# Row statistics of the second normalisation moved from the feed-forward stage into the attention stage, and two small steps of the feed-forward stage given to other engines

## The chip, the cores and the metric

The kernel runs on one core of a Trainium2 chip. The metric is the device time of one execution in microseconds, and lower is better. The kernel before takes 1919.89 us, the median of three runs (1918.67 to 1920.64).

## What is computed

64 images of 3x224x224 and 32 text tokens each are embedded, attended and passed through a feed-forward block:

```python
h = concat([patch_embed(x), text_embed(x_txt)])          # 64 x (196 + 32) x 192, float32
h = h + attention(layernorm(h))                          # 12 heads of 16, causal, q = k = v
h = h + bitlinear(gelu(bitlinear(layernorm(h), w1, g1)), w2, g2)    # 192 -> 768 -> 192

def bitlinear(x, w, g):
    xn = x * rsqrt(mean(x * x) + 1e-6) * g               # one root per row
    scale = 127 / clip(max(abs(xn)), 1e-5)               # one maximum per row
    xq = round(xn * scale) / scale                       # 8-bit values
    return xq @ ternary(w).T
```

The change concerns the last line of the model. Its first bitlinear needs, for every row of h, the mean and variance of the layernorm (the second one of the block), from which one root serves both the layernorm and the rmsnorm, and the largest absolute value of (h - mean) * g1. Its second bitlinear needs the sum of squares of the gelu's 768 outputs, a root of it, and their largest absolute value after g2.

## The kernel before

The rows h of all 64 images stay in SBUF (h_all). An image is 228 rows, held as two tiles of 112 and 116 partitions. The program has a setup, then an **attention stage** over the images, then a **feed-forward stage** over the images; the second starts when the last image's attention is added (semaphore s_h2). There is no scheduler: every engine runs its own list, written out by hand as a function step_images or ffn_step for one image, unrolled at both ends and put in a loop of two images in between. An engine takes its list strictly in order, so an instruction that waits holds up all behind it.

**Attention stage.** Step n of each engine works on four images at once: scores and values of image n, queries of n+1, patch statistics and first layernorm of n+2, patch matmuls of n+3, and the projection of n-1.
- PE (step_images from L1240 on): scores 0, square_turn (L1135, releases DVE's front), queries, scores 1, project(n-1), scores 2, values 0 and values 1 (L1228), a piece of the patches (L1072), score rounds, and so on. values g waits until POOL has cleared the later keys of group g.
- DVE: front(n+2) (L682 to L716) with, inside it, normalise(n-1) (L748), the split of the queries (L725, L727) and add_attention(n-1) (L754); then three maxima (L738) and the reciprocal of the denominators (L743).
- POOL: patch_roots (L454), clear_later of group 0 (L469, two instructions), sides (L435, L438), clear_later of group 1, norm_roots (L459), clear_later of group 2, add_squares (L449, four instructions).

**Feed-forward stage.** Step i of each engine:
- DVE ffn_step (L807 to L874), for image m = i+1: bn_stats and bn_aggr (L820, L824), the variance (L828), the centred and weighted rows v1 (L838), their maxima (L843); for image i-1 the mean of gelu squares (L832), the maxima of v2 (L857); for image i-3 the output rows (L850); then one chain of five small instructions for both quantisers (L863 to L867), each waiting for the one ahead, and last the rounding of v1 to q1 (L874).
- ACT: copy of the turned q1 (L1015), both tiles of q2 (L1003), gelu (L1024), copy of the turned q2 (L1032), squares of the gelu (L1038).
- POOL: one root of four numbers per row, for both normalisations (L512), then g2 times gelu in eight instructions (L524).
- PE: turn_first (L1303), ffn_second (L1333) of image i-2, ffn_first (L1314) of i+1, turn_second (L1325) of i-1.

Of the kernel before, what the change touches and what calls it, by code (L numbers as in the profile page):

```python
# [9 lines left out]
ALU = mybir.AluOpType  # L10
# [29 lines left out]
READY1, READY2 = 36, 52  # L40
# [12 lines left out]
def build(nc, x, x_txt, gamma, beta, tok_w, tok_b, table, pos, carry, qkv_w, qkv_b,  # L53
          proj_w, proj_b, w1, g1, w2, g2, cf, cb, out):
    ctx = ExitStack()
    with ctx:
# [28 lines left out]
        ln_st = sb("ln_st", [128, 32])  # L85
# [69 lines left out]
        v1 = part(xpix[0][:, :], 384, 2 * DIM).rearrange("p (t d) -> p t d", t=2)  # L155
# [73 lines left out]
        f_var = sem("mean_squares_ready")  # L229
        f_r1 = sem("inverse_roots_ready")  # L230
        f_q1 = sem("first_quantised")
# [7 lines left out]
        f_q2 = sem("second_quantised")  # L239
# [15 lines left out]
        V_SETUP, T_SETUP = 69, 9  # L255
# [162 lines left out]
        def _(pool):  # L418
# [42 lines left out]

            zero = pool.to_reg(0.0)
# [32 lines left out]

            step_images(-2, 1, 1, old=False)
            step_images(-1, 0, 2, old=False)
            step_images(0, 1, 2)
            step_images(1, 0, 3)
# [6 lines left out]
            step_images(IMAGES - 1, 0, None, newer=False, newest=False)  # L506

            def ffn_step(i, b, new=True, mid=True):

                if new or mid:  # L510
                    pool.wait_ge(f_var, i + 2)
                    nc.gpsimd.tensor_tensor(ff_st[:, b, 20:24], ff_st[:, b, 16:20], expo[:, 0:4],  # L512
                                            ALU.pow).then_inc(f_r1, 1)
                if not (isinstance(i, int) and (i < 0 or i >= IMAGES)):
                    after(pool, f_q2, i - 1)
                    for tile, P in enumerate((TA, TB)):
                        pool.wait_ge(f_g, 2 * i + tile + 1)
                        if tile == 0:
                            pool.wait_ge(f_r1, i + 2)
                        else:  # L520
                            pool.wait_ge(f_v2, 2 * i + 1)
                        for lo in range(0, HIDDEN, HIDDEN // 4):
                            cols = slice(lo, lo + HIDDEN // 4)
# [10 lines left out]
            with pool.Fori(2, PAIRS - 1) as t:  # L534
                for b in range(2):
                    ffn_step(2 * t + b, b)
# [882 lines left out]
```

## Time and profile before

| | |
|---|---|
| median of three runs | 1919.89 us |
| the profiled execution | 1918.11 us, of which the span of its instructions is 1916.4 us |
| busy share of the span | PE 84%, DVE 72%, ACT 61%, POOL 57% |
| PE in 40 slices (tenths) | 0539999999999999999999999999556666666666 |
| DVE in 40 slices | 3635666666666666666666666666289999999996 |
| POOL in 40 slices | 5035555555555555555555555554177777777775 |
| granted TensorE clock | 1.0 of full speed in the attention stage, a mean of 0.65 in the feed-forward stage |

How to read it: each digit of the slices is the busy share of 1/40 of the span, in tenths (9 is 90% or more). Setup ends near 100 us, the attention stage near 1389 us, and the rest is the feed-forward stage. DVE is the VectorE, ACT the ScalarE, POOL the GpSimd engine, PE the TensorE; PEld is PE's loading of weights, which overlaps the matmuls. An engine's busy share says how much work it has, not whether it sets the pace: for that one looks at who waits for whom.

### The profile page before, as it was taken

Reading aid. Unit: us, or ns where it says so; the run is one execution under the profiler, and the core shown is the slowest. Engines: PE = TensorE matmul, PEld = TensorE weight load, DVE = VectorE, ACT = ScalarE, POOL = GpSimd, SP = SyncE. Lnnn points to the kernel's source line nnn. Section 1 sums busy time; section 2 is a strip of 40 time slices with the busy share of each in tenths; the row PEclk is TensorE's granted clock in tenths of the full one; section 3 lists DMA queues with packets and bytes.
Section 4 is the critical chain, followed back from the end, with each engine's and each line's share of the span. In section 5 each row is a group of like instructions: output and inputs, shape, how many; then the busy total and the mean of one; then the engine's idle time right before and its main releaser. Section 6 shows DMA issues by size and latency. Waiting matters only on the chain.

```text
span 1916.4 us, 50514 instructions
## 1 busy us (share of the span) xinstructions
PE 1614.7 (84%) x16574; PEld 1363.0 (71%) x16574; DVE 1371.2 (72%) x3151; ACT 1171.3 (61%) x1830; POOL 1089.9 (57%) x1503
## 2 busy tenths in 40 slices
PE   0539999999999999999999999999556666666666
PEld 0438888888888888888888888887445555555555
DVE  3635666666666666666666666666289999999996
ACT  1124555555555555555555555555278888888887
POOL 5035555555555555555555555554177777777775
PEclk9969999999999999999999999999666666666665
DMA  8564656565656565656565656561000000000000
GB/s 103 137 116 69 100 78 99 79 100 78 100 79 100 78 99 80 100 79 99 80 100 78 99 80 100 79 99 26 24 12 22 22 22 22 22 22 22 22 22 26
DMA packets 159967, 132.96 MB, mean 69 GB/s; under 512 B 32558, under 2 KB 151040, under 8 KB 159808
## 3 DMA queue, kind: packets, MB, share of 16 engines
q1 hardware_dynamic: 159168, 131.00, 44.0%
q0 software_dynamic: 768, 1.57, 0.5%
q8 instruction: 17, 0.28, 0.1%
q14 instruction: 14, 0.11, 0.0%
HBM read 118.32 MB, written 11.91 MB: 68 GB/s over the span
## 4 chain that ended last, share of the span: by engine, by line
PE 70%; DVE 14%; issue 5%; SPq 4%; ACT 3%; DMA 2%; POOL 1%; DVEq 1%; ACTq 0%; POOLq 0%
PE ps L1072 24%; PE ps L1154 8%; PE ps L1237 7%; PE ps L1228 7%; DVE ff_st L857 4%; PE ps L1184 4%; PE ps L1216 3%; PE ps L1189 3%; PE ps L1210 3%; PE ps L1314 3%; PE ps L1333 2%; DVE xpix L838 2%; PE ps L1145 2%; PE ps L1135 1%; PE ps L1168 1%
## 5 line engine op out<-in xcount | busy, mean ns | idle before, releaser
L1072 PE MATMUL ps<-w_eff,xpix 118*112 118x193 f32 (+1 forms) x2048 | 457.2, 362 | 21.0 <-POOL side L438 20.4
L1072 PEld LDWEIGHTS ps<-w_eff,xpix 118*112 118x112 f32 (+1 forms) x2048 | 387.8, 253 | 39.8 <-issue 32.8
L915 ACT ACTIVATE probs<-ps,isw 116x688 f32<-116x688 f32 x384 | 298.7, 830 | 175.6 <-PE ps L1216 175.6
L449 POOL TENSOR_TENSOR xsq<-xsq 118x784 f32<-118x784 f32 (+2 forms) x192 | 221.8, 1155 | 293.6 <-ACT xsq L909 283.5
L738 DVE TENSOR_REDUCE nmax<-ps 116x12 bf16<-116x1344 f32 (+2 forms) x192 | 302.2, 1574 | 108.7 <-PE ps L1189 103.8
L524 POOL TENSOR_TENSOR xpix<-probs,g_b 112x192 f32<-112x192 f32 (+1 forms) x512 | 296.5, 609 | 109.0 <-ACT probs L1024 99.7
L469 POOL TENSOR_SCALAR_AFFINE_SELECT probs<-probs 116x464 f32<-116x464 f32 x384 | 268.4, 717 | 46.5 <-ACT probs L915 31.0
L682 DVE TENSOR_SCALAR front_st<-ps 112x1 f32<-112x1 f32 (+1 forms) x128 | 18.3, 152 | 229.2 <-PE ps L1135 218.1
L1314 PE MATMUL ps<-w1t,xpix 96*112 96x384 f16 (+1 forms) x512 | 160.7, 488 | 14.5 <-ACT xpix L1015 13.3
L1154 PE MATMUL ps<-xnT,wq_pad 97*128 97x228 f32 (+1 forms) x768 | 166.0, 365 | 0.0
L1303 PE MATMUL ps<-ident_h,xpix 112*96 112x112 f16 (+1 forms) x256 | 34.9, 281 | 152.9 <-DVE xpix L874 152.9
L943 ACT ACTIVATE aux<-ps 128x344 bf16<-128x344 bf16 x64 | 29.3, 457 | 214.4 <-PE ps L1198 214.4
L1237 PE MATMUL ps<-wp_pad,aT 128*112 128x192 f32 (+1 forms) x768 | 144.5, 339 | 11.7 <-DVE aT L748 11.7
L454 POOL TENSOR_TENSOR front_st<-front_st,expo 128x2 f32<-128x2 f32 x64 | 45.0, 703 | 190.9 <-DVE front_st L690 179.1
L909 ACT ACTIVATE xsq<-xpix,consts 118x1176 f32<-118x1176 f32 x64 | 145.6, 2275 | 0.0
L1154 PEld LDWEIGHTS ps<-xnT,wq_pad 97*128 97x128 f32 (+1 forms) x768 | 142.2, 192 | 2.9
L1024 ACT ACTIVATE probs<-ps,ff_st 112x768 f32<-112x768 f32 (+1 forms) x128 | 112.9, 899 | 47.6 <-PE ps L1314 46.2
L1228 PE MATMUL ps<-probs,vaug 112*32 112x228 f32 (+1 forms) x3072 | 140.0, 314 | 2.1 <-POOL probs L469 1.3
L1303 PEld LDWEIGHTS ps<-ident_h,xpix 112*96 112x96 f16 (+1 forms) x256 | 23.8, 168 | 165.7 <-issue 95.8
L1314 PEld LDWEIGHTS ps<-w1t,xpix 96*112 96x112 f16 (+1 forms) x512 | 100.2, 206 | 54.4 <-issue 15.3
L1237 PEld LDWEIGHTS ps<-wp_pad,aT 128*112 128x112 f32 (+1 forms) x768 | 124.6, 182 | 16.0 <-DVE aT L748 12.0
L1333 PE MATMUL ps<-w2t,xpix 128*112 128x192 f16 (+1 forms) x768 | 121.4, 338 | 4.7 <-ACT xpix L1032 4.7
(160 smaller groups left out, 3393.3 us busy)
## 6 DMA issues: line engine op xcount, KB each, us to landing
xpix<-in_x SPq DMA_DIRECT2D x192, 196.0 KB
xpix<-in_x SPq DMA_DIRECT2D x192, 195.1 KB
rden<-den_rows SPq DMA_DIRECT2D x256, 85.5 KB, 2.2
out<-xpix SPq DMA_DIRECT2D x64, 87.0 KB
out<-xpix SPq DMA_DIRECT2D x64, 84.0 KB
xpix<-in_x SPq DMA_DIRECT2D x128, 34.1 KB
xpix<-in_x SPq DMA_DIRECT2D x128, 34.0 KB
den<-o_sb SPq DMA_DIRECT2D x256, 2.7 KB
```

The costliest lines, as they stand in the source:

```text
L449: nc.gpsimd.tensor_tensor(out_, a, b, ALU.add).then_inc(s_ssq, 1)
L469: nc.gpsimd.affine_select(both, both, [[0, 2], [0, 2], [1, TB]], ALU.is_ge, zero, base=0, channel_multiplier=-1).then_inc(s_causal, 1)
L524: last = nc.gpsimd.tensor_tensor(v2[0:P, b, tile, cols], gel[0:P, b, tile, cols], g2_b[0:P, cols], ALU.mult)
L738: V.tensor_reduce(dst, src, AX_X, ALU.max, negate=True).then_inc(s_mx, 1)
L909: A(xsq[0:HI, 1:7, :], pixels[:, 1:7, :], ACT.Square, scale=mult_root[0:HI, 1:2]).then_inc(s_sq, 1)
L915: A(probs[0:TB, g, 2 * e:2 * e + 2, :], ps[0:TB, 4 + 2 * e:6 + 2 * e, 0:SK], ACT.Exp, scale=isw[0:TB, 7:8]).then_inc(s_p, 1)
L1072: last = MM(ps_tok[tile][0:P, :], src, w_eff[0:HI, o, :], start=(o == 0), stop=(o == OFFS - 1))
L1154: last = MM(ps_q[:, g, :], wq_pad[0:K, c, g, :], xnT[0:K, c, :], start=(c == 0), stop=(c == 1))
L1228: last = MM(ps_o[32 * j:32 * j + 32, g, lo:TOK], vaug[0:K, tile, PER * g + j, :], probs[0:K, g, j, at:end], start=(tile == 0), stop=(tile ...
L1237: last = MM(ps[0:P, 1, tile * 256:tile * 256 + DIM], aT[:, g, lo:lo + P], wp_pad[:, g, :], start=(g == 0), stop=(g == GROUPS - 1))
L1314: last = MM(ps[0:P, 2 + 2 * tile + half, 0:HIDDEN // 2], q1T[0:HALF, tile, c, 0:P], w1t[0:HALF, c, half * (HIDDEN // 2):(half + 1) * (HIDD ...
L1333: last = MM(ps[0:P, 1, tile * 256:tile * 256 + DIM], q2T[:, tile, c, 0:P], w2t[:, c, :], start=(c == 0), stop=(c == NCH - 1))
```

## The change

1. **In the attention stage** DVE ends each step with a new function measure(n-1): bn_stats, bn_aggr, the variance, a copy of the mean, the centred rows v1 and their maxima for the image whose attention has just been added. POOL gets row_roots(n-2), a root of two numbers, between patch_roots and the first clear_later.
2. **Between the stages** five small instructions on DVE work out the first quantiser's scales of all images at once.
3. **In the feed-forward stage** DVE no longer has L820, L824, L828, L832 and L843; v1 is computed again (centre), q1 is rounded before the second chain instead of behind it, and the chain is of two numbers per row instead of four. The second tile of q2 is rounded on DVE (quantise_second) instead of ACT. POOL adds the epsilon and takes the gelu's root itself, behind its eight products (gelu_roots); the division by 768 moves into ACT's squares as a scale. v1 gets a buffer of its own.

PE's list stays as it is, save that turn_second waits for the two tiles of q2 apart.

```diff
-            def step_images(n, par, count, old=True, newer=True, newest=True):
+            def step_images(n, par, count, prev=True, old=True, newer=True, newest=True):
                 if newer:
                     patch_roots(n + 2)
+                if prev:
+                    row_roots(n - 2)
                 if old:
                     clear_later(n, 0)
...
+            row_roots(IMAGES - 2)
+            row_roots(IMAGES - 1)
+
+            def weight(n, b):
+                after(pool, f_q2[0], n - 1)
+                after(pool, f_q2[1], n - 1)
+                for tile, P in enumerate((TA, TB)):
+                    pool.wait_ge(f_g, 2 * n + tile + 1)
+                    for lo in range(0, HIDDEN, HIDDEN // 4):
+                        cols = slice(lo, lo + HIDDEN // 4)
+                        last = nc.gpsimd.tensor_tensor(v2[0:P, b, tile, cols], gel[0:P, b, tile, cols],
+                                                       g2_b[0:P, cols], ALU.mult)
+                    last.then_inc(f_v2, 1)
+
+            def gelu_roots(n, b):
+                pool.wait_ge(f_ssq, 2 * n + 2)
+                apart(pool)
+                nc.gpsimd.tensor_scalar(ff_st[:, b, 18:20], gel_sum[:, b, :], EPS_RMS, None,
+                                        ALU.add).then_inc(f_var, 1)
+                pool.wait_ge(f_var, n + 1)
+                nc.gpsimd.tensor_tensor(ff_st[:, b, 20:22], ff_st[:, b, 18:20], expo[:, 0:2],
+                                        ALU.pow).then_inc(f_r1, 1)
+
...
+            for filled in (mean2, rms, peak):
+                step(V.memset(filled[:, :], 1.0))
...
+            def measure(n):
+
+                def chain(ins, k):
+                    ins.then_inc(s_mean2, 1)
+                    dve.wait_ge(s_mean2, n * 3 + k)
+
+                dve.wait_ge(s_h2, n + 1)
+                apart(dve)
+                for tile, P in enumerate((TA, TB)):
+                    last = V.bn_stats(ln_st[0:P, 20 + 6 * tile:26 + 6 * tile], h_all[0:P, hcols(n, tile)])
+                chain(last, 1)
+                apart(dve)
+                for tile, P in enumerate((TA, TB)):
+                    last = V.bn_aggr(ln_st[0:P, 34 + 2 * tile:36 + 2 * tile], ln_st[0:P, 20 + 6 * tile:26 + 6 * tile])
+                chain(last, 2)
+                after(dve, s_rms, n)
+                V.tensor_scalar(ln_st[:, 32:34], ln_st[:, 35:38:2], 1.0 + EPS_RMS,
+                                EPS_LN * EPS_RMS, ALU.mult, ALU.add).then_inc(s_var2, 1)
+                V.tensor_copy(mean2[:, bass.ds(n * 2, 2)], ln_st[:, 34:38:2])
+                for tile, P in enumerate((TA, TB)):
+                    last = V.scalar_tensor_tensor(v1[0:P, tile, :], h_all[0:P, hcols(n, tile)],
+                                                  ln_st[0:P, 34 + 2 * tile:35 + 2 * tile], g1_b[0:P, :],
+                                                  ALU.subtract, ALU.mult)
+                chain(last, 3)
+                for tile, P in enumerate((TA, TB)):
+                    last = V.tensor_reduce(peak[0:P, bass.ds(n * 2 + tile, 1)], v1[0:P, tile, :], AX_X, ALU.max,
+                                           apply_absolute_value=True)
+                last.then_inc(s_peak, 1)
...
+                if prev:
+                    measure(n - 1)
...
+            links[:] = [0, IMAGES * V_FRONT]
+            dve.wait_ge(s_peak, IMAGES)
+            dve.wait_ge(s_rms, IMAGES)
+            link(V.tensor_tensor(peak[:, :], rms[:, :], peak[:, :], ALU.mult))
+            link(V.tensor_scalar(peak[:, :], peak[:, :], 1e-5, None, ALU.max))
+            link(V.reciprocal(inv_peak[:, :], peak[:, :]))
+            V.tensor_scalar(step1[:, :], peak[:, :], isw[:, 4:5], None, ALU.mult)
+            link(V.scalar_tensor_tensor(scale1[:, :], inv_peak[:, :], 127.0, rms[:, :], ALU.mult, ALU.mult))
+            dve.sem_inc(f_sc1, 1)
+
+            F_LINKS = 4
...
+            def centre(n):
+
+                after(dve, f_q1, n)
+                for tile, P in enumerate((TA, TB)):
+                    ins = V.scalar_tensor_tensor(v1[0:P, tile, :], h_all[0:P, hcols(n, tile)],
+                                                 mean2[0:P, bass.ds(n * 2 + tile, 1)], g1_b[0:P, :],
+                                                 ALU.subtract, ALU.mult)
+                ins.then_inc(f_v1, 1)
...
+            def quantise_second(n, b):
+                dve.wait_ge(f_sc, n + 1)
+                after(dve, f_t2, n)
+                V.tensor_scalar(q2[0:TB, 1, :], v2[0:TB, b, 1, :], ff_st[0:TB, b, 39:40], MAGIC16, ALU.mult,
+                                ALU.add).then_inc(f_q2[1], 1)
...
+            def ffn_step(i, b, new=True, mid=True, last_=True):
+
+                if new:
+                    centre(i + 1)
+                if last_:
+                    final(i - 3, 1 - b)
+                if mid:
+                    peaks(i - 1, 1 - b)
+                if new:
+                    quantise_first(i + 1)
+                if mid:
+                    second_scales(i - 1, 1 - b)
+                    quantise_second(i - 1, 1 - b)
```

How the lists move at three places (rows of the programs' own order; a line number of the changed kernel lies some lines below that of the kernel before):

POOL, one attention step, before (front_st, ln_st and rms hold statistics, expo the exponent, probs the probabilities, side and xpix pixels):

```order
L454 TENSOR_TENSOR front_st<-front_st,expo 128x2
L469 AFFINE_SELECT probs<-probs 116x2x232 x2
L435 COPY side<-xpix 54x14x13
L438 COPY side<-xpix 54x14x13
L469 AFFINE_SELECT probs<-probs 116x2x232 x2
L459 TENSOR_TENSOR ln_st<-ln_st,expo 128x2
L469 AFFINE_SELECT probs<-probs 116x2x232 x2
```

and with the change:

```order
L466 TENSOR_TENSOR front_st<-front_st,expo 128x2
L476 TENSOR_TENSOR rms<-ln_st,expo 128x2
L486 AFFINE_SELECT probs<-probs 116x2x232 x2
L447 COPY side<-xpix 54x14x13
L450 COPY side<-xpix 54x14x13
L486 AFFINE_SELECT probs<-probs 116x2x232 x2
L471 TENSOR_TENSOR ln_st<-ln_st,expo 128x2
L486 AFFINE_SELECT probs<-probs 116x2x232 x2
```

The new root stands between the patch root and the first clearing.

DVE, the end of one attention step and the start of the next, with the change (before, L757 is followed at once by L701; nmax are the score maxima, v is v1, mean is mean2):

```order
L757 TENSOR_REDUCE nmax<-ps 116x4
L785 BN_STATS ln_st<-h_all 112x6
L785 BN_STATS ln_st<-h_all 116x6
L789 BN_AGGR ln_st<-ln_st 112x2
L789 BN_AGGR ln_st<-ln_st 116x2
L792 TENSOR_SCALAR ln_st<-ln_st 128x2
L794 COPY mean<-ln_st 128x2
L796 SCALAR_TENSOR_TENSOR v<-h_all,ln_st,g_b 112x192
L796 SCALAR_TENSOR_TENSOR v<-h_all,ln_st,g_b 116x192
L801 TENSOR_REDUCE peak<-v 112x1
L801 TENSOR_REDUCE peak<-v 116x1
L701 TENSOR_SCALAR front_st<-ps 112x1
```

The ten instructions from L785 to L801 were not there.

DVE, the end of one feed-forward step and the head of the next, before (xpix is v1 or q1, ff_st statistics):

```order
L874 TENSOR_SCALAR xpix<-xpix,ff_st 112x192
L874 TENSOR_SCALAR xpix<-xpix,ff_st 116x192
L820 BN_STATS ff_st<-h_all 112x6
L820 BN_STATS ff_st<-h_all 116x6
L824 BN_AGGR ff_st<-ff_st 112x2
L824 BN_AGGR ff_st<-ff_st 116x2
L828 TENSOR_SCALAR ff_st<-ff_st 128x2
L832 TENSOR_SCALAR ff_st<-gel_sum 128x2
L838 SCALAR_TENSOR_TENSOR xpix<-h_all,ff_st,g_b 112x192
L838 SCALAR_TENSOR_TENSOR xpix<-h_all,ff_st,g_b 116x192
L843 TENSOR_REDUCE ff_st<-xpix 112x1
L843 TENSOR_REDUCE ff_st<-xpix 116x1
```

and with the change (xpix<-v is q1, probs<-xpix is q2, xpix<-ps the output rows):

```order
L882 TENSOR_SCALAR xpix<-v,scale 112x192
L882 TENSOR_SCALAR xpix<-v,scale 116x192
L907 TENSOR_TENSOR ff_st<-ff_st 128x2
L908 TENSOR_SCALAR ff_st<-ff_st 128x2
L909 RECIPROCAL ff_st<-ff_st 128x2
L911 TENSOR_SCALAR ff_st<-ff_st,isw 128x2
L912 SCALAR_TENSOR_TENSOR ff_st<-ff_st 128x2
L918 TENSOR_SCALAR probs<-xpix,ff_st 116x768
L873 SCALAR_TENSOR_TENSOR v<-h_all,mean,g_b 112x192
L873 SCALAR_TENSOR_TENSOR v<-h_all,mean,g_b 116x192
L890 SCALAR_TENSOR_TENSOR xpix<-ps,ff_st,h_all 112x192
L890 SCALAR_TENSOR_TENSOR xpix<-ps,ff_st,h_all 116x192
```

Eight instructions (L820 to L832 and L843) are gone from the head of the step, the rounding of q1 (L882) has moved ahead of the chain, and the rounding of q2 (L918) stands at the end.

## Rows read from the trace of the kernel before

Times are microseconds from the start of the span unless marked ns. A timeline row gives start, length, engine, line, operation, output<-inputs, shapes, how many instructions were merged (xN), and in brackets how long the engine had been idle and what ended that.

**Rows 1.** Busy time, granted clock and DMA, two stretches (columns: PE, PEld, DVE, ACT, POOL, PEclk).
```profile
400.00:1300.00 900.00, 899.55 (x10378) 772.32 (x10375) 622.42 (x1269) 522.92 (x752) 499.78 (x658) 1.00 0.62 90
1450.00:1890.00 440.00, 300.95 (x1997) 245.14 (x1996) 404.40 (x1159) 380.61 (x662) 322.96 (x497) 0.65 0.07 22
```

**Rows 2.** The page, part 5: the values matmuls and who held them up.
```profile
L1228 PE MATMUL ps<-probs,vaug 112*32 112x228 f32 (+1 forms) x3072 | 140.0, 314 | 2.1 <-POOL probs L469 1.3
```

**Rows 3.** Timeline of POOL, one attention step (start, length in us).
```profile
1038.72 0.70 POOL L454 TENSOR_TENSOR front_st<-front_st,expo 128x2 f32<-128x2 f32 x1 [2.91 <-DVE front_st L690]
1039.39 1.81 POOL L469 TENSOR_SCALAR_AFFINE_SELECT probs<-probs 116x464 f32<-116x464 f32 x2
...
1041.93 0.49 POOL L438 COPY side<-xpix 54x182 f32<-54x182 f32 x1 [0.16 <-POOL side L435]
1042.66 1.15 POOL L469 TENSOR_SCALAR_AFFINE_SELECT probs<-probs 116x464 f32<-116x464 f32 x2 [0.24 <-POOL side L438]
```

**Rows 4.** Timeline of PE's weight loads, same step.
```profile
1043.27 0.57 PEld L1228 LDWEIGHTS ps<-probs,vaug 112*32 112x32 f32 x16
```

**Rows 5.** Timeline of DVE, end of one attention step and start of the next.
```profile
1033.30 1.05 DVE L738 TENSOR_REDUCE nmax<-ps 116x4 bf16<-116x912 f32 x1
1037.70 0.16 DVE L682 TENSOR_SCALAR front_st<-ps 112x1 f32<-112x1 f32 x1 [3.35 <-PE ps L1135]
...
1039.20 0.86 DVE L748 TENSOR_TENSOR aT<-o_sb,rden 128x684 f32<-128x684 f32 x1
1039.98 1.44 DVE L699 SCALAR_TENSOR_TENSOR h_all<-tok_t,front_st,bw 112x192 f32 x2
```

**Rows 6.** Timeline of POOL during DVE's gap.
```profile
1031.52 3.62 POOL L449 TENSOR_TENSOR xsq<-xsq 118x784 f32<-118x784 f32 x3 [4.38 <-ACT xsq L909]
1035.21 0.60 POOL L449 TENSOR_TENSOR ssq_sb<-xsq 118x196 f32<-118x196 f32 x1
```

**Rows 7.** Timeline of PE, feed-forward stage.
```profile
1599.66 2.80 PE L1314 MATMUL ps<-w1t,xpix 96*112 96x384 f16 x8 [0.92 <-ACT xpix L1015]
1602.26 1.35 PE L1325 MATMUL ps<-ident_h,probs 112*128 112x112 f16 x12
...
1613.10 0.61 PE L1303 MATMUL ps<-ident_h,xpix 112*96 112x112 f16 x4 [2.37 <-DVE xpix L874]
...
1615.43 1.85 PE L1314 MATMUL ps<-w1t,xpix 96*112 96x384 f16 x8
1617.12 0.77 PE L1325 MATMUL ps<-ident_h,probs 112*128 112x112 f16 x12
```

**Rows 8.** Timeline of ACT, feed-forward stage.
```profile
1611.07 1.37 ACT L1032 ACTIVATE xpix<-ps 128x672 f16<-128x672 f16 x2
...
1613.96 0.60 ACT L1015 ACTIVATE xpix<-ps 96x224 f16<-96x224 f16 x2
```

**Rows 9.** Timeline of DVE, one feed-forward step.
```profile
1605.42 0.60 DVE L820 BATCH_NORM_STATS2 ff_st<-h_all 112x6 f32 x2
...
1606.99 0.15 DVE L832 TENSOR_SCALAR ff_st<-gel_sum 128x2 f32<-128x2 f32 x1
...
1607.82 0.61 DVE L843 TENSOR_REDUCE ff_st<-xpix 112x1 f32<-112x192 f32 x2
```

**Rows 10.** Line L843: all its instructions, first and last start.
```profile
L843 DVE TENSOR_REDUCE ff_st<-xpix x128: 340/348/354, 1390.9 to 1887.1; 112x1 f32<-112x192 f32 x64, 116x1 f32<-116x192 f32 x64
```

**Rows 11.** Groups by line and shape, DVE, 1450 to 1890 us.
```profile
L874 DVE TENSOR_SCALAR xpix<-xpix,ff_st 112x192 f16<-112x192 f32 x55 | 31.3, 570 | 1.9
...
L874 DVE TENSOR_SCALAR xpix<-xpix,ff_st 116x192 f16<-116x192 f32 x55 | 16.9, 307 | 0.0
```

**Rows 12.** Timeline of DVE in the setup: the widest rounding to half precision.
```profile
75.64 0.76 DVE L631 TENSOR_SCALAR xpix<-xpix 128x1152 f16<-128x1152 f32 x1
```

**Rows 13.** Groups by line, POOL, 1450 to 1890 us.
```profile
L524 POOL TENSOR_TENSOR xpix<-probs,g_b 112x192 f32<-112x192 f32 (+1 forms) x442 | 255.6, 608 | 96.9 <-ACT probs L1024 89.0
L512 POOL TENSOR_TENSOR ff_st<-ff_st,expo 128x4 f32<-128x4 f32 x55 | 67.5, 1226 | 21.0 <-DVE ff_st L832 11.9 <-POOL xpix L524 9.1
```

More of the change, by code:

```diff
@@ L238, in build @@
         f_v2 = sem("gelu_weighted")
-        f_q2 = sem("second_quantised")
+        f_q2 = [sem(f"second_quantised{i}") for i in range(2)]
         f_t2 = sem("second_transposed")
@@ L506, in _ @@
             step_images(IMAGES - 1, 0, None, newer=False, newest=False)
[L508 to L523, printed above, removed]
-                            last = nc.gpsimd.tensor_tensor(v2[0:P, b, tile, cols], gel[0:P, b, tile, cols],
-                                                           g2_b[0:P, cols], ALU.mult)
-                        last.then_inc(f_v2, 1)
-                    pool.wait_ge(f_v2, 2 * i + 2)
@@ new lines, in gelu_roots @@
+            def gelu_roots(n, b):
[6 more added lines that the diff above has]
+                                        ALU.pow).then_inc(f_r1, 1)
+            weight(0, 0)
@@ L535, in _ @@
+            gelu_roots(0, 0)
+            weight(1, 1)
+            gelu_roots(1, 1)
+            with pool.Fori(1, PAIRS) as t:
                 for b in range(2):
-                    ffn_step(2 * t + b, b)
-            ffn_step(IMAGES - 2, 0)
-            ffn_step(IMAGES - 1, 1, new=False)
-            ffn_step(IMAGES, 0, new=False)
+                    weight(2 * t + b, b)
+                    gelu_roots(2 * t + b, b)
         @block.vector
@@ new lines, in centre, with quantise_first @@
+            def centre(n):
[5 more added lines that the diff above has]
+                ins.then_inc(f_v1, 1)
+            def quantise_first(n):
+                dve.wait_ge(f_v1, n + 1)
+                after(dve, f_t1, n)
+                for tile, P in enumerate((TA, TB)):
+                    ins = V.tensor_scalar(q1[0:P, tile, :], v1[0:P, tile, :], scale1[0:P, bass.ds(n * 2 + tile, 1)],
+                                          MAGIC16, ALU.mult, ALU.add)
+                ins.then_inc(f_q1, 1)
@@ new lines, in final, with peaks @@
+            def final(n, b):
+                dve.wait_ge(f_m2, n + 1)
+                after(dve, f_out, 32 * n)
+                for tile, P in enumerate((TA, TB)):
+                    end = V.scalar_tensor_tensor(y[0:P, tile, :], ps[0:P, 1, tile * 256:tile * 256 + DIM],
+                                                 ff_st[0:P, b, 42 + tile:43 + tile], h_all[0:P, hcols(n, tile)],
+                                                 ALU.mult, ALU.add)
+                end.then_inc(f_y, 1)
+            def peaks(n, b):
+                dve.wait_ge(f_v2, 2 * n + 2)
+                for tile, P in enumerate((TA, TB)):
+                    ins = V.tensor_reduce(ff_st[0:P, b, 26 + tile:27 + tile], v2[0:P, b, tile, :], AX_X, ALU.max,
+                                          apply_absolute_value=True)
+                flinks[:] = [0, n * F_LINKS]
+                flink(ins)
@@ L888, in _ @@
             ffn_step(IMAGES - 1, 1, new=False)
[L889 removed]
+            ffn_step(IMAGES, 0, new=False)
             ffn_step(IMAGES + 1, 1, new=False, mid=False)
```

136 lines of the change are left out of this document (46 added, 90 removed).

## The prediction

> **What bounds the kernel now.** I read the busy time by stage first, then who waits for whom, then one step of each stage in order of time. In the attention stage PE is busy 899.55 of 900 us at the full clock; DVE has 622 us of work there and POOL 500 [rows 1]. So PE sets the pace, work added to DVE or POOL is free as long as PE waits for none of it, and each us that PE waits per image costs about 60 us. In the feed-forward stage no engine is full: per 440 us DVE has 404, ACT 381, POOL 323, PE 301 at a mean clock of 0.65 [rows 1]. There DVE's step is what PE waits for: before turn_first it stands idle 2.37 us until L874 has written q1 [rows 7]. The step takes (1887.1-1390.9)/63 = 7.87 us, since L843 runs twice per image [rows 10].
>
> **The attention stage, POOL.** Today PE waits for POOL's clearings a total of 1.3 us in the run [rows 2], which looks like room and isn't. In the step shown, POOL starts the patch root at 1038.72 and ends the second clearing of group 1 at 1042.66+1.15 = 1043.81, with almost no idle time between [rows 3]. PE's 16 weight loads of values 0 end at 1043.27+0.57 = 1043.84, and those of values 1 need that clearing [rows 4]. The slack is 0.03 us. The new root goes between the patch root and the first clearing. It is the same instruction as the patch root, 0.70 us [rows 3]. Part of it is covered. The first pair of clearings takes 1.81 us where the second takes 1.15 [rows 3]: it overlaps DVE's L748 (1039.20 to 1040.06) and L699 (1039.98 to 1041.42, 1.44 us for two) [rows 5]. I read this as DVE and POOL taking turns at SBUF. The root too will wait for L748's end, so POOL is ready for the first clearing at about 1040.06+0.60 = 1040.65 instead of being let through at about 1040.0. By the same turns the pair ends some 0.7 later; a tenth I take off, since the sides behind it then meet none of L699. That makes 0.6 us of wait for PE per image. Ends: 0.45, if the pair, met by less of DVE's work, shrinks by another 0.15 towards 1.15; and 1.05, if POOL's root and DVE shut each other out wholly: L699's two instructions then start half a root, 0.35, later than with a clearing in their way, the clearings behind them too, and nothing is regained (0.70+0.35). I take the low part of that span because of the next row.
>
> L748 starts at 1039.20, inside the patch root (1038.72 to 1039.42), and takes 0.86 us for 684 elements a row, in line with L738's 1.05 for 912 (which reads no SBUF), so the root doesn't keep it out in its last 0.2 us [rows 3, 5]. The Trainium skill (SBUF — State Buffer, Who interferes with whom) says that DVE and GpSimd hold their shared port pair for a whole instruction, the other fully blocked. By that rule L699's first instruction waits for the whole new root, the clearing waits for L699, and the stage would lose the upper end. The trace does not agree for this root, as far as L748's 0.86 us show.
>
> The root meets patch_roots and the clearings in steps 2 to 61: 60 x 0.6 = +36 us (27 to 63).
>
> **The attention stage, DVE.** measure stands where DVE waits for PE: L738 ends at 1034.35, L682 starts at 1037.70, a gap of 3.35 us [rows 5]. Its instructions are those of the feed-forward head. There the head runs from L820's start at 1605.42 to L843's end at 1607.82+0.61 = 1608.43, 3.0 us with its waits for POOL [rows 9]; L832 goes out of it and the copy of the mean comes in, 0.1 each. So 3.0 us fit with 0.3 to spare. In the gap POOL runs its square sums until 1035.81 [rows 6]; DVE's variance may wait for the last of them. I count 0 for DVE. If measure took 3.9, the excess of 0.5 would go through the front, POOL's chain and the clearings to PE. POOL's square sums end 1.9 us before L682, which needs them through PE, so some tenths of delay there cost nothing.
>
> **The feed-forward stage, DVE.** Removed: the head up to L832's start, 1606.99-1605.42 = 1.57 us, L832's 0.15 and L843's 0.61, less 0.1 of overlap: 2.2 us [rows 9]. Added: q2's tile of 116x768. L874 on 192 elements takes 0.307 without a wait [rows 11], the setup's rounding of 1152 elements 0.76 [rows 12]; between them 768 gives 0.58. L874's first tile takes 0.570, 0.26 more than the second, which is the wait for POOL [rows 11]; so 0.85. DVE's own step becomes 7.87-2.2+0.85 = 6.5 us.
>
> **POOL.** Eight products of 0.608 are 4.9 us [rows 13]. The root of two numbers is 0.70 [rows 3] instead of 1.23 [rows 13]. The addition of an epsilon has no row on POOL. Below, zero; above, 0.60, the addition of 196 columns [rows 6]; three such additions of 784, 392 and 196 columns take 3.62 [rows 6], some 2 ns a column, so two columns cost about 0.2. With 0.3 for hand-overs POOL needs 6.1 us: no bound, even with 0.6 it is 6.5. What it does is add about 1 us to the way from the squares to q2's scales, which have a whole step of slack.
>
> **ACT and PE, late next.** The change leaves a loop untouched: q1's copy on ACT, ffn_first and turn_second on PE, q2's copy and the squares on ACT, next q1's copy. From the start of L1032 to the start of L1015 ACT needs 1613.96-1611.07 = 2.89 us, L1015 itself 0.60 [rows 8], the hand-over to PE 0.1. PE from L1314's start to L1325's end takes 1599.66 to 1603.61 = 3.95 us at half clock, and 1615.43 to 1617.89 = 2.46 where the clock rose to full in between [rows 7]. A mean of 0.65 is 30% of the time at full clock, giving 3.95x0.7+2.46x0.3 = 3.5. The loop is 2.89+0.60+0.1+3.5 = 7.1 us. That is the new step: the loop is longer than DVE's 6.5 and POOL's 6.1, and ACT, busy 381x7.87/440 = 6.8 us a step [rows 1], loses one of its eight long instructions. Ends: 7.54 with the half clock throughout, and 6.5, DVE's own. Gain: 64 x (7.87-7.1) = -49 us (-21 to -88).
>
> **Edges.** Three fills in the setup, 0.4 us. Between the stages the last measure (3.0) and five chained small instructions (0.16 each as L682 [rows 5], 0.9 with hand-overs) come before the first q1, where the head of image 0 was; the second q1 then follows faster. The last image waits 1 us longer for POOL and saves half of ACT's rounding. Together +0.5.
>
> **Sum.** 36-49+0.5 = -12.5 on the profiled execution's 1918.1: 1905.6. The median of the runs is 1.8 above it, so 1907. A measurement of this kernel can tell about 0.2% (4 us) from no change.
>
> **Rivals.**
> - *PE waits longer in attention* (slower). POOL's root and L699 exclude each other, or measure outgrows its gap of 3.35 us. From a wait of 0.81 us on, the stage's loss exceeds the other's gain. With 1.05: 63-49+0.5 = +14, or 1934. For: slack of 0.03 us and DVE within 0.3 of its gap. Against: L748 wasn't held up by the patch root. Chance 0.22.
> - *The loop at half clock* (slower). The stage's step is 7.54, the gain 21: +36-21 = +15, or 1935. For: PE would be busier at half clock, with no guarantee of more. Against: today's mean is 0.65. Chance 0.10.
> - *The stage runs at DVE's own 6.5.* The clock rises as PE's idle 2.37 us per step shrinks, and the loop gives way: 36-88 = -52, or 1868. For: the full clock where PE is never idle [rows 1]. Chance 0.13.
> - *The new root is hidden.* The clearings speed up enough that PE doesn't wait: -49, or 1871. Against it the slack of 0.03. Chance 0.08.
>
> **How the numbers follow.** The forecast has 0.47. The forecast's own range is 1892 to 1925 (a wait of 0.45 to 0.8 us, a step of 7.0 to 7.2). The range reaches to the slow cases with 3 us beyond, and to half of the fast ones: 1870 to 1938. Faster: 0.39 of the forecast, and both fast cases, 0.60. Within 0.2%: 0.08 of the forecast and 0.04 of the first rival, 0.12. Slower: the rest, 0.28.
>
> **What would show it.** In attention: PE idle before values 1 by 0.6 us, put down to POOL's clearing; DVE's wait before the front near 0.3 us instead of 3.35; POOL's new root at 0.7 us plus a wait. In the feed-forward stage: a step of 7.1, DVE with idle time of its own, and a granted clock of 0.65 or more. The prediction is wrong if PE doesn't wait in attention, or if the step's limit is POOL.

## The result and the profile after

The changed kernel takes 1938.6 us, the median of 4 runs (1937.7 to 1940.1), against 1919.5 for the kernel before on the same chip: a ratio of 1.010 (95% interval 1.008 to 1.012). It is slower by 19 us where 1907 had been forecast. The profiled execution's span grew from 1916.4 to 1936.2 us, 19.8 us. In the tables below "before" is measured anew on each chip, at 1918 to 1920 us.

Busy time and granted clock of the changed kernel, in the two stretches of [rows 1] (columns as there):

```profile
400.00:1300.00 900.00, 888.76 (x10167) 750.22 (x10167) 701.86 (x1703) 517.19 (x737) 508.07 (x690) 1.00 0.61 88
1450.00:1890.00 440.00, 262.72 (x1981) 217.75 (x1981) 415.13 (x773) 336.85 (x609) 329.30 (x555) 0.78 0.07 22
```

PE has lost 11 of its 900 busy us in the attention stage. In the feed-forward stage DVE is busier than before and PE less, at a granted clock of 0.78 where it had 0.65. Where the 19.8 us lie can be read from first and last starts. The rows are of single lines (busy ns least/median/most, then first and last start): the attention's normalising multiply in the kernel before and after (once per image), and the maxima of the feed-forward stage before and after (twice per image):

```profile
L748 DVE TENSOR_TENSOR aT<-o_sb,rden x64: 857/860/1131, 174.7 to 1383.7; 128x684 f32<-128x684 f32 x64
L857 DVE TENSOR_REDUCE ff_st<-xpix x128: 939/941/952, 1402.5 to 1902.8; 112x1 f32<-112x768 f32 x64, 116x1 f32<-116x768 f32 x64
```

```profile
L767 DVE TENSOR_TENSOR aT<-o_sb,rden x64: 857/861/1016, 175.4 to 1404.8; 128x684 f32<-128x684 f32 x64
L898 DVE TENSOR_REDUCE ff_st<-xpix x128: 932/941/954, 1425.3 to 1923.4; 112x1 f32<-112x768 f32 x64, 116x1 f32<-116x768 f32 x64
```

The attention stage grew from 1209.0 to 1229.4, +20.4 us. The feed-forward stage shrank from 500.3 to 498.1, only -2.2 us (the maxima follow each other at (498.1-0.9)/63 = 7.89 us, before 7.93; the prediction's 7.87 is the same step by another line). What lies ahead, between and behind adds 0.7+1.7-0.8 = +1.6.

**The attention stage.** POOL and DVE around the new root, the clearing that values 1 need, and PE's weight loads there (timeline of the changed kernel: start, length, what the engine was idle for):

```profile
1035.94 0.70 POOL L466 TENSOR_TENSOR front_st<-front_st,expo 128x2 f32<-128x2 f32 x1 [2.96 <-DVE front_st L709]
1036.61 1.21 POOL L476 TENSOR_TENSOR rms<-ln_st,expo 128x2 f32 x1
1037.78 1.15 POOL L486 TENSOR_SCALAR_AFFINE_SELECT probs<-probs 116x464 f32<-116x464 f32 x2
1038.89 0.48 POOL L447 COPY side<-xpix 54x182 f32<-54x182 f32 x1
...
1040.26 1.15 POOL L486 TENSOR_SCALAR_AFFINE_SELECT probs<-probs 116x464 f32<-116x464 f32 x2 [0.24 <-POOL side L450]
```

```profile
1036.35 0.86 DVE L767 TENSOR_TENSOR aT<-o_sb,rden 128x684 f32<-128x684 f32 x1
1037.13 0.74 DVE L718 SCALAR_TENSOR_TENSOR h_all<-tok_t,front_st,bw 112x192 f32 x2
```

```profile
1041.46 0.55 PEld L1280 LDWEIGHTS ps<-probs,vaug 112*32 112x32 f32 x16 [0.50 <-POOL probs L486]
```

The new root waits for L767 and takes 1.21 us. From the patch root to the first clearing there are now 1037.78-1035.94 = 1.84 us, where there were 0.67 [rows 3]: 1.17 more. The pair of clearings takes 1.15 instead of 1.81, since L718 now runs during the root and not during them. From the first pair's start to the second's there are 1040.26-1037.78 = 2.48 us, where there were 1042.66-1039.39 = 3.27 [rows 3]. So of the 1.17 us 0.79 come back, and the pair that values 1 need starts 0.38 us later behind the patch root than before. PE waits for it. In the middle of the stage (from the fifth start of the normalising multiply to the 61st, over 56) the step grew from 19.18 to 19.57 us, by just that 0.38; the steps at the ends lose less, and 20.4 us over 60 steps are 0.34 each.

DVE's added work did fit in its gap, as the step's end shows (0.39 us are left of the 3.35 of [rows 5]):

```profile
1031.36 0.61 DVE L785 BATCH_NORM_STATS2 ln_st<-h_all 112x6 f32 x2
...
1033.85 0.61 DVE L801 TENSOR_REDUCE peak<-v 112x192 f32 x2
1034.85 0.16 DVE L701 TENSOR_SCALAR front_st<-ps 112x1 f32<-112x1 f32 x1 [0.39 <-PE ps L1187]
```

**The feed-forward stage.** Here stands what the prediction did not have. L882 writes q1, and its first tile is one instruction on 192 columns. The group by shape, DVE, 1450 to 1850 us (busy, mean ns of one, idle before), and one stretch of all engines:

```profile
L882 DVE TENSOR_SCALAR xpix<-v,scale 112x192 f16<-112x192 f32 x51 | 96.9, 1901 | 14.9 <-DVE ff_st L898 14.9
L882 DVE TENSOR_SCALAR xpix<-v,scale 116x192 f16<-116x192 f32 x51 | 15.6, 306 | 0.0
```

```profile
1710.45 4.66 POOL L536 TENSOR_TENSOR xpix<-probs,g_b 112x192 f32<-112x192 f32 x8 [0.15 <-ACT probs L1075]
1711.42 2.70 DVE L882 TENSOR_SCALAR xpix<-v,scale 112x192 f16<-112x192 f32 x2 [0.29 <-DVE ff_st L898]
...
1714.17 0.61 PE L1355 MATMUL ps<-ident_h,xpix 112*96 112x112 f16 x4 [3.58 <-DVE xpix L882]
```

The first tile takes 1901 ns in the mean, the second 306; before they took 570 and 307 [rows 11]. Here the pair starts at 1711.42, while POOL's second product of eight runs, and ends at 1714.12, when POOL is in its seventh; PE idles 3.58 us for it, where it idled 2.37 before [rows 7]. One image in three escapes (0.63 us for the tile), and there the step is 7.0 us; in the others, with 2.5 to 2.7 us for the tile, it is 8.3 to 8.6. Called "hold-out" below: an instruction of DVE that is kept waiting while several of POOL's pass.

### The profile page after: what moved, and what is told of

It reads as the page before. It is cut to its first block, busy times and chain, and to the rows that moved or that the text cites. A ratio compares the mean times of both kernels' runs of the same rounds, so it can differ in the third digit from the quotient of the medians.

```text
span 1936.2 us, 51421 instructions
## 1 busy us (share of the span) xinstructions
PE 1582.7 (82%) x16574; PEld 1325.7 (68%) x16574; DVE 1508.7 (78%) x3341; ACT 1126.5 (58%) x1766; POOL 1121.9 (58%) x1629
## 4 chain that ended last, share of the span: by engine, by line
issue 30%; PE 29%; POOL 17%; DVE 14%; SPq 4%; DMA 2%; POOLq 2%; ACT 2%; DVEq 1%; ACTq 0%
PE ps L1124 13%; POOL probs L486 6%; POOL xsq L461 5%; DVE ff_st L898 4%; PE ps L1280 3%; PE ps L1236 2%; PE ps L1385 2%; PE ps L1366 2%; PE ps L1241 2%; POOL side L450 2%; POOL side L447 1%; DVE v L873 1%; DVE xpix L890 1%; DVE ff_st L908 1%; DVE xpix L882 1%
## 5 line engine op out<-in xcount | busy, mean ns | idle before, releaser
L757 DVE TENSOR_REDUCE nmax<-ps 116x12 bf16<-116x1344 f32 (+2 forms) x192 | 302.7, 1577 | 140.9 <-PE ps L1241 134.1
L536 POOL TENSOR_TENSOR xpix<-probs,g_b 112x192 f32<-112x192 f32 (+1 forms) x512 | 314.8, 650 | 118.4 <-ACT probs L1075 117.2
L486 POOL TENSOR_SCALAR_AFFINE_SELECT probs<-probs 116x464 f32<-116x464 f32 x384 | 230.0, 616 | 25.9 <-POOL side L450 14.6
L1280 PE MATMUL ps<-probs,vaug 112*32 112x228 f32 (+1 forms) x3072 | 151.1, 315 | 15.8 <-POOL probs L486 15.8
L1366 PE MATMUL ps<-w1t,xpix 96*112 96x384 f16 (+1 forms) x512 | 134.7, 424 | 24.7 <-ACT xpix L1067 24.7
L1075 ACT ACTIVATE probs<-ps,step 112x768 f32<-112x768 f32 (+1 forms) x128 | 110.6, 898 | 73.3 <-PE ps L1366 73.3
L882 DVE TENSOR_SCALAR xpix<-v,scale 112x192 f16<-112x192 f32 (+1 forms) x128 | 129.9, 1054 | 17.2 <-DVE ff_st L898 17.0
L1366 PEld LDWEIGHTS ps<-w1t,xpix 96*112 96x112 f16 (+1 forms) x512 | 86.4, 177 | 55.4 <-issue 22.1
```

Source lines behind the costliest of these rows:

```text
L486: nc.gpsimd.affine_select(both, both, [[0, 2], [0, 2], [1, TB]], ALU.is_ge, zero, base=0, channel_multiplier=-1).then_inc(s_causal, 1)
L536: last = nc.gpsimd.tensor_tensor(v2[0:P, b, tile, cols], gel[0:P, b, tile, cols], g2_b[0:P, cols], ALU.mult)
L757: V.tensor_reduce(dst, src, AX_X, ALU.max, negate=True).then_inc(s_mx, 1)
L882: ins = V.tensor_scalar(q1[0:P, tile, :], v1[0:P, tile, :], scale1[0:P, bass.ds(n * 2 + tile, 1)], MAGIC16, ALU.mult, ALU.add)
L1280: last = MM(ps_o[32 * j:32 * j + 32, g, lo:TOK], vaug[0:K, tile, PER * g + j, :], probs[0:K, g, j, at:end], start=(tile == 0), stop=(tile ...
L1366: last = MM(ps[0:P, 2 + 2 * tile + half, 0:HIDDEN // 2], q1T[0:HALF, tile, c, 0:P], w1t[0:HALF, c, half * (HIDDEN // 2):(half + 1) * (HIDD ...
```

## The experiments

Three theories were open. T1: POOL's new root costs the attention stage its 20 us. T2: the hold-out of q1's first tile eats the gain of the feed-forward stage, and something in the change made it possible. Rival: the step of 7.9 us has another limit (the loop of ACT and PE, or POOL), and the hold-out is only seen because there is room.

### Each half alone

First the attention part on the feed-forward stage of before, then the reverse, with measure() and row_roots() taken out (the means, roots and first maxima then stay at 1):

> The kernel before, with only the attention stage of the change: measure on DVE and row_roots on POOL run for every image, and the feed-forward stage is that of before and takes its own statistics (what measure finds is not used). Both theories of the feed-forward stage expect the same here: the stage's loss of 0.39 us a step stays whole, so 1919.5 + 20.5 + 1 (three fills, and the last measure) = 1941. If the loss came from an interplay with the new feed-forward stage, it would be 1920.

> The change without measure and row_roots: the feed-forward stage uses means, roots and maxima that stay at 1, so the outputs are not the reference's. Held-out theory (the gain of the feed-forward stage is eaten by the first tile of q1, which POOL's products keep out of SBUF for four or five products in two images of three): the stage keeps its 7.82 us a step, attention returns to 19.18, total 1938.6 - 21 - 3 = 1915, with the first tile of q1 at 2.5 us in two images of three. Rival (the moved statistics or their buffers slow the feed-forward stage): under 1890.

Measured: 1943.1 us, ratio 1.012 (1.010 to 1.014), and 1916.5 us, ratio 0.999 (0.998 to 1.000). The parts add up to within 3 us: one costs 24 us, the other gains 2.5, and together they cost 19. In the first one's profile the unchanged feed-forward stage happened to run at a granted clock of 0.78, not 0.65 as in [rows 1]:

```profile
1450.00:1890.00 440.00, 267.77 (x1997) 221.04 (x1995) 407.17 (x1162) 376.68 (x664) 327.43 (x499) 0.78 0.07 22
```

Its stage didn't get shorter for that: from the first maxima to the last it takes 499.9 us, where it took 500.3. So between these two clocks PE's speed was no term of the step of before.

### The root behind the clearings

```diff
-                if prev:
-                    row_roots(n - 2)
                 if old:
                     clear_later(n, 0)
...
                 if old:
                     clear_later(n, 2)
+                if prev:
+                    row_roots(n - 2)
```

> The change with row_roots moved behind the last clearing of the step, where POOL waits over 4 us for ACT's squares. Theory that attention's loss is POOL's root ahead of the clearings of group 1: the step returns from 19.57 to 19.2 us and PE's wait for POOL at the values goes to nothing, total 1938.6 - 21 = 1918. Rival (DVE's measure, which leaves 0.4 us of its gap of 3.35, delays PE): the step stays at 19.57, total 1938.

Measured: 1916.0 us, ratio 0.999 (0.998 to 1.000), 22.6 us less than the change, with all of its work done. PE is full again in 400 to 1300 us:

```profile
400.00:1300.00 900.00, 899.51 (x10378) 770.77 (x10377) 747.46 (x1737) 523.85 (x752) 531.61 (x704) 1.00 0.62 89
```

In the middle of the attention stage the step is back at 19.18 us; the whole stage takes 1211.4 us, 2.4 more than before. T1 is shown: all but these 2.4 us come from the root's place, and neither from its own work nor from DVE's measure().

### What is held out, and where

The first guess was that only q1's form of instruction is held out, and that a small instruction with two inputs ahead of it would bring it into step with POOL's products.

```diff
+                V.tensor_tensor(meet[:, 0:2], expo[:, 0:2], expo[:, 2:4], ALU.mult)
                 for tile, P in enumerate((TA, TB)):
                     ins = V.tensor_scalar(q1[0:P, tile, :], ...
```

> The change with one more DVE instruction, a product of two columns from two SBUF inputs, right before the first tile of q1. Held-out theory (an instruction of the 2-port form that comes to POOL's products in the middle of one is kept out for four or five of them, one that comes just behind a product's start gets in after it): the small instruction waits for at most one product, q1 then comes 0.1 to 0.2 us behind a product's start and takes 0.55 to 0.65 in all images; the step falls from 7.82 to about 7.1, total 1938.6 - 45 = 1894. Rival (the ACT and PE loop at half clock sets the step, q1's wait only fills idle time): q1 may get shorter, but the step stays above 7.6 and the total above 1925.

Measured: 1941.7 us (ratio 1.0098 to 1.0132). The 1894 is missed. The rival's number (above 1925) came out, but this doesn't speak for its reason, because the wait had only moved: q1's first tile was held in 2 images, and in 26 of 64 the small instruction waited, up to 2.70 us for 2 columns:

```profile
L882 DVE TENSOR_TENSOR meet<-expo x64: 160/510/2697, 1415.6 to 1914.2; 128x2 f32<-128x2 f32 x64
```

So neither this form of instruction nor its size decides; it looked as if the moment of arrival did. That left two suspects in the diff: the new order of DVE's work, and a line that went with POOL's old function. POOL used to wait for its own four products of tile 0 ahead of tile 1's.

### The dropped wait, more waits, and two other orders

```diff
                     pool.wait_ge(f_g, 2 * n + tile + 1)
+                    if tile == 1:
+                        pool.wait_ge(f_v2, 2 * n + 1)
```

> POOL waits for its own fourth product before it starts the second tile's four, so that its products no longer run all eight back to back. Theory A (first-quantised tile on DVE is kept out as long as POOL's products follow one another, and the step waits for it): its long form falls from 2.5 us to what is left of the first tile's products, about 1.3 us; the feed-forward step falls from 7.82 to 7.2-7.5 us and the time to 1900-1918 us. Rival B (the hold-out is there but something else would bound the step at 7.8): the tile shortens and the time stays at 1938 +- 3. Rival C (the hold-out has nothing to do with POOL's queueing): the long form stays at 2.5 us, 1938.

Next, such a wait behind each of the eight products:

> POOL waits for itself after each of its eight products; each then costs it about 0.1 us more (0.8 us per image, of POOL's 6.4 busy or less). Theory A: DVE gets in within one product, the first quantised tile takes at most 0.9 us in every image, the step comes to 7.1-7.4 us, the time to 1893-1915 us. Rival B (another limit, POOL's own 7.0 us or the ACT and TensorE loop, at 7.6 or more): the tile is short and the time 1925-1940. Rival C: long tiles stay, 1938.

Then two orders of DVE's calls without any wait, peaks, second_scales, quantise_first in the one and quantise_first, peaks, second_scales in the other:

> The only edit puts the first quantisation behind the five small instructions of the scales, the order of the kernel before. Theory A (the new order made it arrive in the middle of a product, with instructions ahead that don't use the contended port): the long form vanishes (0.55 to 0.75 us each), but it again waits for the root and the scales, about 1 us later than where it could run: step 7.5-7.9, time 1920-1940, as before's. Rival D (the long form comes with the second tile of q2 on DVE, not with the order): long tiles stay and the time grows to 1945 or more.

> The only edit puts the first quantisation ahead of the two maxima (which use 1.9 us of DVE), where POOL is mostly idle or at its root. Theory A: the first quantised tiles take 0.31 to 0.7 us in every image and TensorE gets them some 2 us sooner; the small instructions of the scales now arrive mid-product and some are held up to 2.5 us, which delays q2 only. If TensorE's transposes of q2 have that slack: step 7.0-7.4, time 1888-1912. If not: 7.6-7.9 and 1925-1942. Rival B: 1938 with both in time.

| run | us | ratio to before | step, us | longest of q1's tile, and of the first scales |
|---|---|---|---|---|
| the change | 1938.6 | 1.008 to 1.012 | 7.89 | 2.68 and 2.72 |
| wait behind the 4th product | 1870.4 | 0.972 to 0.977 | 6.85 | 0.72 and 0.55 |
| wait behind every product | 1894.7 | 0.985 to 0.990 | 7.19 | 0.73 and 0.59 |
| q1 behind the scales | 2028.8 | 1.052 to 1.059 | 9.32 | 0.73 and 2.75 |
| q1 ahead of the maxima | 1876.4 | 0.974 to 0.981 | 6.82 | 0.50 and 2.71 |

The first scales are the first two instructions of the chain. The step is the distance of the maxima, (last start - first - 0.9)/63. One wait on one line gives 68 us, far more than the 21 to 39 expected. In its profile q1's first tile gets in at once, again while POOL's second product runs (POOL's four to each tile are merged in the rows):

```profile
1648.74 0.55 DVE L884 TENSOR_SCALAR xpix<-v,scale 112x192 f16<-112x192 f32 x2 [0.30 <-DVE ff_st L900]
```

```profile
1647.79 2.50 POOL L538 TENSOR_TENSOR xpix<-probs,g_b 112x192 f32<-112x192 f32 x4 [0.18 <-ACT probs L1077]
1650.50 3.00 POOL L538 TENSOR_TENSOR xpix<-probs,g_b 116x192 f32<-116x192 f32 x4 [0.21 <-POOL xpix L538]
```

The wait costs POOL 0.21 us. Waits behind all eight products also shorten the tile, and their 1894.7 us, as expected, are 44 less than the change's, but 24 more than with the single wait. The order of before, which I expected to be harmless, is the worst without the wait, and both its expectations are missed: now the scales' second instruction is held out in 37 of 64 images (median 2704 ns) and one of its neighbours in 10 others, and they stand on the way to q1 and q2. With q1 ahead of the maxima the hold-out strikes the scales (median 1473 ns for the first of them), and q2 has room for it; the time lies 12 us below the expected range. The rival falls: the step had no other limit above 6.85.

### The kernel before without its wait

```diff
-                        else:
-                            pool.wait_ge(f_v2, 2 * i + 1)
```

> The kernel before, with one wait taken away: POOL's wait for its own four products of the first tile ahead of the second tile's, the line that the change also dropped. Theory A (that wait is what lets DVE in, and its loss made the hold-outs): instructions of DVE that come behind the maxima or the centring are now kept out for 2.5 to 2.7 us in part of the images, the step grows from 7.86 to 8.2 us or more, the time to 1940-2030. Rival B (the hold-out comes from the new order of DVE's work, and the wait plays no part in before): 1919 +- 3, no instruction of DVE but the maxima over 1 us.

Measured: 2014.0 us, ratio 1.050 (1.048 to 1.052), a step of 9.41 us. Nothing else of the change is in this kernel. The second instruction of the chain, on 4 columns, before and in this run:

```profile
L864 DVE TENSOR_SCALAR ff_st<-ff_st x66: 169/504/524, 1392.1 to 1904.0; 128x4 f32<-128x4 f32 x66
```

```profile
L862 DVE TENSOR_SCALAR ff_st<-ff_st x66: 170/2637/2720, 1390.8 to 1996.3; 128x4 f32<-128x4 f32 x66
```

That settles the cause: the dropped wait, which orders nothing that needs ordering, is worth 95 us in the kernel before and 68 us in the change.

### Put together, and the tile on DVE priced

The wait between the tiles with the root behind the clearings; then q1 ahead of the maxima as well; then, in place of that, both of q2's tiles on ACT:

> The change with POOL's own wait between the tiles and the row root behind the clearings. The two parts lie in separate stages, so the gains of the two runs (68 and 23 us) should add: 1870.4 - 22.6 = 1848 (1844-1852). Rival: where the late root had worked only by chance of alignment, 1855-1870.

> As the run before it, with the first quantisation also ahead of the two maxima. Theory: with the gap the step is set by DVE's own work of 6.4 to 6.5 us and its waits at the port; taking the first tiles to where POOL is at its root saves 0.3 us of port waits per image: step 6.5-6.85, time 1828-1850. Rival: the step of 6.85 is not DVE's any more but the loop of ACT and TensorE, 1848 +- 4; or the small instructions of the scales are held instead (1.45 us in the run without the gap) and it comes to 1850-1860.

> The change with the gap and the late root, and both tiles of q2 on ACT as before the change: this prices the move of one tile to DVE. Theory A (by the sum on record: the loop of ACT and TensorE would be 0.6 to 0.7 us longer, DVE's own 0.6 to 0.8 shorter): ACT's 6.0 us busy grow to 6.6, step 7.3-7.5, time 1880-1890. Rival (DVE is the bound now): step 6.3-6.8, time 1815-1845, and the move of the tile costs time.

Measured: 1848.7 us (ratio 0.962 to 0.966), 1850.3 (0.962 to 0.966) and 1851.3 (0.963 to 0.967). The first is the best kernel of the study, 3.6% faster than before, and it hits its sum. The other two lie within 3 us of it (the second at its rival's 1848 +- 4), so both expectations of the third fail: the tile's move neither costs nor brings more than 3 us. Busy time in 1450 to 1780 us, of the first and the third run:

```profile
1450.00:1780.00 330.00, 215.18 (x1740) 176.74 (x1741) 308.53 (x676) 285.14 (x530) 307.67 (x482) 0.85 0.09 25
```

```profile
1450.00:1780.00 330.00, 254.31 (x1744) 199.08 (x1744) 296.15 (x630) 324.86 (x583) 294.20 (x485) 0.75 0.09 25
```

With the tile on DVE, DVE and POOL are busy 93% each and ACT 86%; with it on ACT, ACT is busy 98%. The step is the same, 6.82 and 6.81 us. I read this as one limit in place of another; no run shows what ends the step of 6.8.

### Where the wait has to stand

```diff
+                        if tile == 0 and lo == HIDDEN // 4 * 1:
+                            last.then_inc(f_part, 1)
+                            pool.wait_ge(f_part, n + 1)
```

In the second of these two runs the condition is tile == 1, which puts the wait behind the sixth product.

> The change with POOL's wait for its own second product of the first tile (a semaphore of its own), six of eight products still back to back. In the hold-outs so far DVE's instruction arrived while the second product ran and got in four or five products later. Theory A (it gets in where POOL's queue is drained by a wait, wherever that is): arrivals in the second product get in at its end, q1's first tile takes at most 0.9 us, step 6.9-7.1, time 1870-1885, unless instructions behind the wait are held in their turn. Theory B (what counts is how many products follow without a wait: six in a row are enough for a hold-out of some 2 us): part of the instructions that arrive in the third or fourth product take 1.5 us or more, time 1885-1935.

> The same wait, behind the sixth product. Theory A (DVE gets in where the wait drains POOL's queue): what arrives in the second product is held for about four products, until the sixth ends, so the long form stays at 2.2 to 2.7 us, step 7.7-7.9, time 1925-1940. Theory B (any stretch of at most six products lets DVE in sooner): the long form falls under 1 us and the time to 1870-1890.

Measured: 1871.7 us (ratio 0.974 to 0.978) and 1894.8 (0.986 to 0.991). The rows of q1's instruction in the two:

```profile
L886 DVE TENSOR_SCALAR xpix<-v,scale x128: 306/318/739, 1417.3 to 1847.6; 112x192 f16<-112x192 f32 x64, 116x192 f16<-116x192 f32 x64
```

```profile
L886 DVE TENSOR_SCALAR xpix<-v,scale x128: 306/318/1828, 1416.7 to 1866.5; 112x192 f16<-112x192 f32 x64, 116x192 f16<-116x192 f32 x64
```

The longest of q1's instructions takes 0.74 us with the wait behind the 2nd product, 0.72 behind the 4th, 1.83 behind the 6th, 2.68 with none. Theory A, that DVE gets in only where the wait is, fits the first run, but would have left the sixth-product run at 1925 or more. Theory B has the direction there, but its tile under 1 us isn't met and its 1870 to 1890 is missed by 5 us.

The starts and ends of all products and of the DVE instructions that take over 1.2 us show where DVE gets in. With eight products in a row 40 of 41 hold-outs in the change, and all 48 that began in the second product in the kernel before without its wait, end within 0.2 us of the seventh product's start; so do the 60 that began in the fourth with q1 ahead of the maxima. With the wait behind the 6th, 15 of the 16 that began in the second end within 0.2 us of the fifth's start. Both are two products ahead of the end of the unbroken run, and with the wait behind the 4th the same count gives the third product, which fits the 0.72 us. It isn't the whole rule: with the wait behind the 2nd, six products still follow each other, 57 DVE instructions arrive in the second of these six, and none takes over 0.53 us. How a wait that is still ahead lets DVE in earlier is open; no run here shows what POOL has taken on at that moment.

## Why the prediction was wrong

The time lies 0.6 us above the range's upper end of 1938, and the sign was wrong. By the steps:

- **POOL's root makes PE wait: right; 0.6 us was mis-sized.** Measured 0.34 a step in the mean (0.38 in the middle of the stage) and 20 us in all, for 36 predicted, below the lower end of 27. The prediction had the root wait for L748 and end some 0.65 late, and took off a tenth for what comes behind. The root took more (1.17 until the clearings start), but the pair of clearings fell all the way from 1.81 to 1.15, and what follows it by another 0.13. The lower end had counted only 0.15 beyond the tenth. The 1.15 of a pair that meets nothing stood in [rows 3]: once the root covers L699, the first pair is such a pair.
- **measure() fits in DVE's gap: right**, with 0.39 us to spare for 0.3 expected.
- **The upper end for attention.** It followed a rule of the Trainium skill (SBUF — State Buffer, Who interferes with whom), that who issues first holds the pair of ports for its whole instruction. Row L476 agrees with it for L767 and the root. It isn't the whole of it: L718's two instructions and the root overlap, and the clearings gave the time back.
- **The step goes to 7.1 us: the failed step.** The gain was 2 us, not 49. Two of its premises were wrong. First, q1's wait at SBUF was carried over from [rows 11] as 0.26 us, "which is the wait for POOL", as if it belonged to the instruction. It belonged to POOL's products being broken in the middle, and the change dropped the line that broke them. In the kernel before, 43 instructions of DVE start in the second product and none takes over 0.52 us. The prediction costed POOL's eight products and the epsilon, and gave the dropped wait no line at all. Second, the limit behind it, the loop of ACT and PE, did not stand at 7.1: with the hold-out gone the step is 6.85, at a granted clock of 0.85 (wait behind the 4th product) and of 0.75 (behind the 2nd) alike. PE's 3.5 us in that loop took the 2.46 of [rows 7] for the full clock, but in 1615.43 to 1617.89 us the clock granted was 0.84 in the mean. What ends the step of 6.85 is not shown. With the wait kept, the change is at 1870, close to the rival of DVE's own 6.5 (1868), but by luck: 22 us were lost in attention where the rival had 36, and 68 gained in the feed-forward stage where it had 88.
- **q2's tile on DVE, 0.85 us**: it took 0.62 or 0.85. It is worth nothing measurable for the step, as its price on the best kernel shows. **POOL's epsilon** took 0.217 us, estimated at 0.2.
- **The granted clock** of 0.65 or more: it was 0.78, and beside the point, since the feed-forward stage of before ran at 0.78 without being faster.
- **The rivals.** The one that came nearest in time (1934, PE waits longer in attention) is not what happened: PE waited less than forecast. No rival named a DVE instruction held by several of POOL's.

## What to carry to other kernels

Read each wait that a diff drops as an instruction of its own, also one that no data need: ask which engine's unbroken run of instructions it split, and which other engine got at SBUF because of it. A duration read from a trace includes the waits that its neighbours gave it; when the neighbours change, bound it by the length of the other engine's whole queue, not by the row. And when a serial engine gets one more instruction, look for the place in its list behind the last one that somebody waits for: the same root cost 20 us in front of the clearings and, with all of measure(), at most 2.4 us behind them.

## What the runs showed of the hardware

- DVE can be kept out by more than one instruction of POOL. With eight products of 192 columns in a row, 0.55 us apart, DVE instructions of 2, 4 and 192 columns that arrived in the second product and were held took 2.3 to 2.9 us (one 1.8) instead of 0.16 to 0.31. That held for forms with one input and with two. The Trainium skill's rule on the pair of ports (SBUF — State Buffer, Who interferes with whom) speaks of one whole instruction; these runs show four to five.
- In most of them DVE's instruction had arrived while the second product ran, but not all such arrivals were held: 48 of 62 in the kernel before without its wait, 41 of 66 in the change (over 1.2 us, the maxima not counted). With q1 ahead of the maxima 60 arrived in the fourth product, and all were held, taking 1.45 to 1.53 us. With eight products in a row, arrivals in the first were over within 0.75 us, but for two (2.92 us, in the run with the small instruction). The maxima of 768 columns (tensor_reduce, one input, 931 to 955 ns in all runs) were never held.
- POOL's wait for its own second, fourth or every product ended this (one such wait costs POOL 0.2 us); behind the sixth it only shortened it. A wait on a semaphore of ACT's that had already been reached did not end it: it stands between the two tiles in the change too, and in the stretch shown ACT was done at 1711.16 us, 1.5 us before the fifth product started at 1712.64.
